# Gathering stage: splitting the second bank of weights into two rounded parts in every fourth unit

## The chip, the cores and the metric

The kernel runs on one core of a Trainium2 chip. The metric is the device time of one execution in microseconds; what is compared is the median over runs. The core has TensorE (PE, matrix products), VectorE (DVE), ScalarE (ACT), GpSimd (POOL) and SyncE (SP, which here only issues DMAs). Each engine runs its own instructions in order, and they wait for one another by semaphores. SBUF is the working memory; PSUM is the memory that TensorE writes to.

## The reference

A decoder layer for 64 sequences of 128 tokens with 128 features: self-attention, cross-attention, and a soft mixture of experts. The stage that is changed belongs to the last part:

```python
# x: 8192 tokens x 128; 64 experts (n) with 32 slots (p) each
logits = (einsum('tzd,ed->tze', x, phi_w) + phi_b).reshape(t, z, n, p)
D = softmax(logits, axis=3)                # over the slots of one expert
X_tilde = einsum('tznp,tzd->npd', D, x)    # gathers 2048 slots of 128
...
Y = einsum('tznp,npH->tzH', softmax(logits, axis=2), Y_tilde)
```

The gathering stage computes `logits`, `D` and `X_tilde`, and stores half of the logits for the last stage.

## The kernel before

Stages run one after the other: attention, cross-attention, a short preparation, **gathering** (`gather_slots`, about 603 to 1052 us of the profile), the experts, and the mixing stage.

Gathering goes over 64 tiles of 128 tokens, and over each in two **units**: unit `u` takes tile `u // 2` and half `u % 2` of the 2048 slots. So there are 128 units, and each has 1024 slots in two **banks** of 512 (16 experts each). A software pipeline with lags is written out by hand: iteration `k` works on units `k` to `k - 4`, each engine in the order of its own loop.

- TensorE: logits of unit `k` (L849, six matmuls of rounded fp32r operands: high times high, low times high, high times low, for two banks); subtraction of the maxima of unit `k - 1` in PSUM (L856, two); for unit `k - 4` the products that gather tokens into slots, summed over all tiles in four PSUM banks `slots_X`. Of these, bank 1 is one matmul in full fp32 (L863), which the trace records as two instructions. Bank 0 is three fp32r matmuls (L868 to L870), of `x2h`, `x2l` (high and low part of the tokens) and `dh`, `dl` (high and low part of the weights).
- ScalarE: copies the logits to keep, bank 1 and bank 0 (L875); the exponential `e` of unit `k - 1` (L886); for unit `k - 2` the rounded `x2h` (L895, every second unit) and `dh` (L898).
- VectorE: maxima `mx` of both banks of unit `k` (L907, L909); for unit `k - 1` sums `rsum` (L913) and reciprocals `rinv` (L917); every second unit `x2l` (L923).
- GpSimd: `dl` of unit `k - 3` (L932), then the weights `d` of unit `k - 1`, which is `e` times `rinv` (L938, both banks, 1024 columns).

`d` lies in four buffers, `dh` and `dl` in two each. In the names of the trace the stage's own tiles begin with `gather_`. In the attention stage, GpSimd's L210 adds two bands of 128x512 and its L213 adds a constant to four columns; VectorE's L359 works on 128x512 with both inputs in SBUF, and its L330 on 128x512 with one input in PSUM.

Of the kernel before, what the change touches and what calls it, by code (L numbers as in the profile page):

```python
# [18 lines left out]
ALU = mybir.AluOpType  # L19
# [3 lines left out]
F32R = mybir.dt.float32r  # L23
# [32 lines left out]
def reach(eng, sem, value):  # L56

    if not isinstance(value, int) or value > 0:
        eng.wait_ge(sem, value)  # L59
# [730 lines left out]
def gather_slots(nc, io, w, psX):  # L790
# [4 lines left out]
    TILES = TOKENS // 128  # L795
    UNITS = 2 * TILES
    KEEPS = 3
    with ExitStack() as ctx:
        st = Store(nc, ctx, "gather")
        mx = [st.sb(f"mx{i}", [128, 2, 16], F32R) for i in range(2)]  # L800
# [3 lines left out]
        dd = [st.sb(f"d{i}", [128, 2, 512]) for i in range(4)]  # L804

        x2h = [st.sb(f"x2h{i}", [128, 128], F32R) for i in range(2)]
        x2l = [st.sb(f"x2l{i}", [128, 128], F32R) for i in range(2)]
        dh = [st.sb(f"dh{i}", [128, 512], F32R) for i in range(2)]
        dl = [st.sb(f"dl{i}", [128, 512], F32R) for i in range(2)]
        keep = [st.sb(f"keep{i}", [128, SLOTS - MADE, 32]) for i in range(KEEPS)]  # L810
        psL = [st.ps(f"L{i}", [128, 2, 512]) for i in range(2)]

# [3 lines left out]
         x_made) = (  # L816
            st.sem(n) for n in ("l_made", "low_max", "mx_ready", "kept", "shifted", "e_ready", "sum_done", "rinv_ready",
                                "d_ready", "d_read", "dh_ready", "dl_ready", "x_made"))
        stored = [st.sem(f"stored{i}") for i in range(KEEPS)]
        block = ctx.enter_context(nc.Block())  # L820

        def units(k, lag):
            return [k - lag] if 0 <= k - lag < UNITS else []

        def rows(u):
            return slice(u // 2 * 128, u // 2 * 128 + 128)
# [14 lines left out]
        @block.tensor  # L841
        def _(pe):
            for k in ORDER:
                for u in units(k, 0):
                    reach(pe, e_ready, u - 1)
                    for n, (xs, ws) in enumerate(((w.xh, w.w1h), (w.xl, w.w1h), (w.xh, w.w1l))):
                        for i in range(2):
                            c = (2 * (u % 2) + i) * 512
                            ins = pe.matmul(psL[u % 2][:, i, :], xs[:, rows(u)], ws[:, c:c + 512],  # L849
                                            start=n == 0, stop=n == 2)  # L850
                    ins.then_inc(l_made, 1)
                for u in units(k, 1):
                    pe.wait_ge(mx_ready, u + 1)
                    pe.wait_ge(kept, 2 * u + 2)
                    for i in range(2):
                        ins = pe.matmul(psL[u % 2][:, i, :], w.neg_ident[:],  # L856
                                        mx[u % 2][:, i, :].unsqueeze(2).to_broadcast([128, 16, 32]), start=False,
                                        stop=True, skip_group_check=True)
                    ins.then_inc(shifted, 1)
                for u in units(k, 4):  # L860
                    t, j, first, last = u // 2, u % 2, u < 2, u >= UNITS - 2
                    pe.wait_ge(d_ready, u + 1)
                    pe.matmul(psX[:, 2 * j + 1, :], w.xres[:, rows(u)], dd[u % 4][:, 1, :], start=first, stop=last)\  # L863
                        .then_inc(d_read, 1)
                    pe.wait_ge(x2l_ready, t + 1)
                    pe.wait_ge(dl_ready, u + 1)
                    out = psX[:, 2 * j, :]
                    pe.matmul(out, x2h[t % 2][:], dh[j][:], start=first, stop=False)  # L868
                    pe.matmul(out, x2h[t % 2][:], dl[j][:], start=False, stop=False)
                    pe.matmul(out, x2l[t % 2][:], dh[j][:], start=False, stop=last).then_inc(x_made, 1)  # L870

        @block.scalar
        def _(act):
            def keep_bank(u, i):
                act.copy(keep[u % KEEPS][:, :, 16 * i:16 * i + 16],  # L875
                         psL[u % 2][:, i, :].rearrange("t (n p) -> t p n", n=16)[:, MADE:SLOTS, :]).then_inc(kept, 1)

            for k in ORDER:
                for u in units(k, 0):
                    act.wait_ge(l_made, u + 1)  # L880
                    reach(act, stored[u % KEEPS], 16 * (u // KEEPS))
                    keep_bank(u, 1)
                for u in units(k, 1):
                    act.wait_ge(shifted, u + 1)
                    reach(act, d_ready, u - 1)
                    act.activation(e[u % 2][:], psL[u % 2][:].rearrange("p i (n s) -> p i n s", n=16), ACT.Exp)\  # L886
                        .then_inc(e_ready, 1)
                for u in units(k, 0):
                    act.wait_ge(low_max, u + 1)
                    keep_bank(u, 0)  # L890
                for u in units(k, 2):
                    t, j = u // 2, u % 2
                    if j == 0:
                        reach(act, x_made, u - 2)
                        act.copy(x2h[t % 2][:], w.xres[:, rows(u)]).then_inc(x2h_ready, 1)  # L895
                    act.wait_ge(d_ready, u + 1)
                    reach(act, x_made, u - 1)
                    act.copy(dh[j][:], dd[u % 4][:, 0, :]).then_inc(dh_ready, 1)  # L898

        @block.vector  # L900
        def _(dve):
            for k in ORDER:
# [15 lines left out]
                for u in units(k, 2):  # L918
                    t = u // 2
                    if u % 2 == 0:  # L920
                        dve.wait_ge(x2h_ready, t + 1)
                        reach(dve, x_made, u - 2)
                        dve.tensor_tensor(x2l[t % 2][:], w.xres[:, rows(u)], x2h[t % 2][:], ALU.subtract)\  # L923
                            .then_inc(x2l_ready, 1)

        @block.gpsimd
        def _(pool):
            for k in ORDER:
                for u in units(k, 3):
                    pool.wait_ge(dh_ready, u + 1)  # L930
                    reach(pool, x_made, u - 1)
                    pool.tensor_tensor(dl[u % 2][:], dd[u % 4][:, 0, :], dh[u % 2][:], ALU.subtract).then_inc(dl_ready, 1)  # L932
                for u in units(k, 1):
                    pool.wait_ge(rinv_ready, u + 1)

                    reach(pool, d_read, u - 3)
                    reach(pool, dl_ready, u - 3)
                    pool.tensor_tensor(  # L938
                        dd[u % 4][:].rearrange("p i (n s) -> p i n s", n=16), e[u % 2][:],
                        rinv[u % 2][:].rearrange("p (i n) -> p i n", i=2).unsqueeze(3).to_broadcast([128, 2, 16, 32]),  # L940
                        ALU.mult).then_inc(d_ready, 1)
# [413 lines left out]
```

## Time and profile before

| | |
|---|---|
| Median of 3 runs | 1550.07 us (1549.28 to 1550.47) |
| The profiled execution | 1551.19 us, its span 1549.0 us |
| Mean granted clock of TensorE | 0.966 of 2.4 GHz |
| Busy in the span: PE, DVE, ACT, POOL | 1387.7, 1164.3, 872.3, 1151.5 us |
| Gathering: GpSimd's L938 and L932 (128 each) | 244.9 us and 165.9 us busy |
| Gathering: VectorE's L913, L907, L909, L917 (128 each) | 156.2, 88.5, 87.0, 45.2 us busy |
| Gathering: TensorE's L863 (256 records) | 130.7 us busy |

How to read the rows further down: times are microseconds from the start of the span, durations of an operation's executions are nanoseconds. PEld is TensorE's loading of weights, which runs beside its matmuls. In brackets behind a timeline row stands the engine's idle time before it and what ended that. A matmul's recorded length is longer than the distance to the next, since matmuls are pipelined; starts are what to compare. A record may start shortly before the engine's last one ends. An execution's recorded length includes time in which it was issued but held up.

### The profile page before, as it was taken

To read this page: it belongs to the slowest core of one execution; us is meant where nothing else is said; L and a number is where in the kernel's file an instruction comes from. 1 tells how busy PE (TensorE), PEld (TensorE's weight loads), DVE (VectorE), ACT (ScalarE), POOL (GpSimd) and SP (SyncE) were. 2 spreads that over 40 slices of the span, in tenths; PEclk is the share of its full clock that TensorE was granted. 3 is DMA by queue.
4 is the path that set the end of the run, shared out by engine and by line. 5 is a ranking of instruction groups with operands and counts; after the bars stand their busy time and mean duration, and the time that the engine had idled before them with its cause. 6 is when DMAs were issued, how large, how long until landed. Compare 5 with 4: busy or idle time off the path is not lost. (4 is left out here: it accounts for less than half of the span.)

```text
span 1549.0 us, 35158 instructions
## 1 busy us (share of the span) xinstructions
PE 1387.7 (90%) x12926; PEld 1114.6 (72%) x12926; DVE 1164.3 (75%) x2389; ACT 872.3 (56%) x1546; POOL 1151.5 (74%) x1028
## 2 busy tenths in 40 slices
PE   5765588888888885999999999996999999999998
PEld 4554466666666653777777777764899999999998
DVE  4997466666666665888888888885778778787885
ACT  3776244444444442676767677762566565655655
POOL 2443466666666652899999999993899999999997
PEclk9897599999999997999999999999999999999999
DMA  5110343333333314222222222221222332232231
GB/s 158 35 40 7 97 118 89 90 90 89 90 90 92 92 41 130 76 76 81 76 82 76 82 75 78 79 75 42 86 79 76 93 84 77 87 93 79 76 92 28
DMA packets 77195, 123.82 MB, mean 80 GB/s; under 512 B 8353, under 2 KB 45794, under 8 KB 77026
## 3 DMA queue, kind: packets, MB, share of 16 engines
q1 hardware_dynamic: 75426, 117.16, 24.2%
q0 software_dynamic: 1088, 4.19, 0.9%
q8 instruction: 104, 1.70, 0.5%
q14 instruction: 65, 0.53, 0.1%
q10 hardware_dynamic: 512, 0.23, 0.1%
HBM read 70.28 MB, written 51.27 MB: 78 GB/s over the span
## 5 line engine op out<-in xcount | busy, mean ns | idle before, releaser
L938 POOL TENSOR_TENSOR gather_d<-gather_e,gather_rinv 128x1024 f32<-128x1024 f32 x128 | 244.9, 1914 | 53.4 <-DVE gather_rinv L917 53.4
L1244 POOL TENSOR_TENSOR mix_c<-mix_e,mix_rinv 128x1024 f32<-128x1024 f32 x128 | 241.0, 1903 | 24.9 <-DVE mix_rinv L1211 24.9
L1171 PEld LDWEIGHTS mix_Y<-kept_phi,mix_cT 128*128 128x128 f32 x2048 | 248.1, 192 | 9.0
L1171 PE MATMUL mix_Y<-kept_phi,mix_cT 128*128 128x128 f32 x2048 | 249.0, 275 | 0.0
L1187 ACT COPY mix_cT<-mix_T 128x1024 f32<-128x1024 f32 x128 | 128.6, 1005 | 170.1 <-PE mix_T L1178 170.1
L1208 DVE TENSOR_REDUCE mix_sums<-mix_e 128x16 f32<-128x1024 f32 x128 | 152.6, 1193 | 85.3 <-ACT mix_e L1191 83.0
L717 POOL TENSOR_TENSOR cross_kd<-cross_pack,kept_consts 128x624 fp32r<-128x624 f32 x128 | 155.3, 1233 | 42.1 <-DMA cross_pack<-cross_halves 40.9
L913 DVE TENSOR_REDUCE gather_rsum<-gather_e 128x32 f32<-128x1024 f32 x128 | 156.2, 1220 | 26.7 <-ACT gather_e L886 26.7
L932 POOL TENSOR_TENSOR gather_dl<-gather_d,gather_dh 128x512 fp32r<-128x512 f32 x128 | 165.9, 1296 | 0.0
L875 ACT COPY gather_keep<-gather_L 128x256 f32<-128x256 f32 x256 | 94.7, 370 | 105.5 <-PE gather_L L849 98.7
L595 ACT ACTIVATE cross_pT<-cross_P 77x1024 f32<-77x1024 f32 x128 | 123.5, 1015 | 49.0 <-PE cross_P L536 49.0
L1178 PE MATMUL mix_T<-kept_consts,mix_c 128*128 128x128 f32 x1024 | 134.6, 275 | 5.1 <-POOL mix_c L1244 5.0
L1255 POOL TENSOR_TENSOR mix_less<-mix_read,mix_high 128x1024 f32<-128x1024 f32 x64 | 122.4, 1913 | 19.3 <-DVE mix_high L1224 19.1
L886 ACT ACTIVATE gather_e<-gather_L 128x1024 f32<-128x1024 f32 x128 | 131.2, 1025 | 8.3 <-PE gather_L L856 0.9
L645 DVE TENSOR_REDUCE cross_mx<-cross_S 128x8 fp32r<-128x624 f32 x128 | 102.9, 804 | 39.5 <-PE cross_S L518 39.5
L863 PE MATMUL slots_X<-gather_d,kept_xres 128*128 128x512 f32 x256 | 130.7, 592 | 0.0
L1178 PEld LDWEIGHTS mix_T<-kept_consts,mix_c 128*128 128x128 f32 x1024 | 117.6, 143 | 6.4 <-POOL mix_c L1244 6.4
L907 DVE TENSOR_REDUCE gather_mx<-gather_L 128x16 fp32r<-128x512 f32 x128 | 88.5, 691 | 32.7 <-PE gather_L L849 23.7
L868 PE MATMUL slots_X<-gather_dh,gather_x2h 128*128 128x512 f32 x128 | 101.3, 792 | 2.9 <-DVE gather_x2l L923 1.5
L723 POOL TENSOR_TENSOR cross_veps<-cross_mv,kept_eps 128x1 f32<-128x1 f32 x64 | 12.1, 189 | 120.8 <-DVE cross_mv L659 120.8
L898 ACT CAST gather_dh<-gather_d 128x512 fp32r<-128x512 f32 x128 | 79.8, 623 | 32.1 <-PE slots_X L870 20.0
L849 PE MATMUL gather_L<-second_w1h,kept_xh 128*128 128x512 f32 x256 | 82.0, 401 | 12.8 <-ACT gather_e L886 9.0
(188 smaller groups left out, 3171.5 us busy)
## 6 DMA issues: line engine op xcount, KB each, us to landing
kept_logits<-gather_keep SPq DMA_DIRECT2D x128, 256.0 KB, 2.0
mix_read<-kept_logits SPq DMA_DIRECT2D x64, 512.0 KB, 3.7
cross_halves<-cross_qk SPq DMA_DIRECT2D x32, 412.0 KB, 2.9
cross_pack<-cross_halves SPq DMA_DIRECT2D x64, 128.0 KB
cross_pack<-cross_halves SPq DMA_DIRECT2D x32, 206.0 KB
cross_pack<-cross_halves SPq DMA_DIRECT2D x64, 78.0 KB
attn_xTg<-in_xT SPq DMA_DIRECT2D x16, 256.0 KB, 2.8
kept_xres<-in_x POOLq DMA_DIRECT2D x4, 1024.0 KB, 12.3
```

Of the source, the lines that this page charges most:

```text
L595: ins = act.activation(pT[n % 2][0:J, hs, :, :], psP[:, hs, :, :], ACT.Exp)
L717: pool.tensor_tensor(kd[n % 2][:, q], keys[:, q].to_broadcast([128, 2, 4, JP]), w.own.unsqueeze(1).unsqueeze(3).to_broadcast([128, 2, 4, J ...
L863: pe.matmul(psX[:, 2 * j + 1, :], w.xres[:, rows(u)], dd[u % 4][:, 1, :], start=first, stop=last)\
L886: act.activation(e[u % 2][:], psL[u % 2][:].rearrange("p i (n s) -> p i n s", n=16), ACT.Exp)\
L913: dve.tensor_reduce(rsum[u % 2][:].rearrange("p (i n) -> p i n", i=2), e[u % 2][:], X, ALU.add)\
L932: pool.tensor_tensor(dl[u % 2][:], dd[u % 4][:, 0, :], dh[u % 2][:], ALU.subtract).then_inc(dl_ready, 1)
L938: pool.tensor_tensor(dd[u % 4][:].rearrange("p i (n s) -> p i n s", n=16), e[u % 2][:], rinv[u % 2][:].rearrange("p (i n) -> p i n", i=2). ...
L1171: ins = pe.matmul(psY[t % 2][:, 0:128], cT[u % 2][:, c, :], w.yk[:, 8 * (u % 2) + c, :], start=(u % 2 == 0 and c == 0), stop=(u % 2 == 1 a ...
L1178: ins = pe.transpose(psT[:, c, :], cc[u % 2][:, 2 * c:2 * c + 2, :], w.ident)
L1187: act.copy(cT[u % 2][:], psT[:]).then_inc(cT_ready, 1)
L1208: dve.tensor_reduce(sums[u % 2][:], e[u % 2][:], X, ALU.add).then_inc(sum_done, 1)
L1244: pool.tensor_tensor(cc[u % 2][:], e[u % 2][:], rinv[u % 2][:].unsqueeze(2).to_broadcast([128, 16, EXPERTS]), ALU.mult)\
```

## The change

In every fourth unit (u = 3, 7, ... 127, all in the second half of their tile) bank 1 is gathered as bank 0 is: ScalarE makes a rounded high part `eh` of the bank's weights, VectorE subtracts it from them and gets the low part `el`, and TensorE does three fp32r matmuls in place of the one in fp32. `eh` and `el` have one buffer each; three semaphores are new. The three matmuls come after those of bank 0.

```diff
@@ gather_slots @@
+    SPLIT = 4
...
+        def split(u):
+
+            return u % SPLIT == SPLIT - 1
...
@@ block.tensor, unit k - 4 @@
                     pe.wait_ge(d_ready, u + 1)
-                    pe.matmul(psX[:, 2 * j + 1, :], w.xres[:, rows(u)], dd[u % 4][:, 1, :], start=first, stop=last)\
-                        .then_inc(d_read, 1)
+                    out = psX[:, 2 * j + 1, :]
+                    if not split(u):
+                        pe.matmul(out, w.xres[:, rows(u)], dd[u % 4][:, 1, :], start=first, stop=last)\
+                            .then_inc(d_read, 1)
...
                     pe.matmul(out, x2l[t % 2][:], dh[j][:], start=False, stop=last).then_inc(x_made, 1)
+                    if split(u):
+                        out = psX[:, 2 * j + 1, :]
+                        pe.wait_ge(el_ready, u // SPLIT + 1)
+                        pe.matmul(out, x2h[t % 2][:], eh[:], start=first, stop=False)
+                        pe.matmul(out, x2h[t % 2][:], el[:], start=False, stop=False)
+                        pe.matmul(out, x2l[t % 2][:], eh[:], start=False, stop=last).then_inc(split_read, 1)
...
@@ block.scalar, after dh of unit k - 2 @@
+                for u in units(k, 3):
+                    if split(u):
+                        reach(act, split_read, u // SPLIT)
+                        act.copy(eh[:], dd[u % 4][:, 1, :]).then_inc(eh_ready, 1)
...
@@ block.vector, after x2l of unit k - 2 @@
+                for u in units(k, 3):
+                    if split(u):
+                        dve.wait_ge(eh_ready, u // SPLIT + 1)
+                        reach(dve, split_read, u // SPLIT)
+                        dve.tensor_tensor(el[:], dd[u % 4][:, 1, :], eh[:], ALU.subtract).then_inc(el_ready, 1)
...
@@ block.gpsimd, before d of unit k - 1 @@
-                    reach(pool, d_read, u - 3)
+                    reach(pool, d_read, straight(u - 3))
+                    reach(pool, el_ready, max(u - 3, 0) // SPLIT)
```

`straight(n)` counts the units among the first `n` that are not split. ScalarE (before `x2h`) and VectorE (before `x2l`) wait for `split_read` too, before they overwrite the tokens' parts.

VectorE's instructions around the end of iteration 6, before. `mx` are the maxima, `rsum` and `rinv` the sums and reciprocals of the softmax:

```order
L913 TENSOR_REDUCE gather_rsum<-gather_e 128x32 [waits gather_rinv_ready,gather_e_ready]
L917 RECIPROCAL gather_rinv<-gather_rsum 128x32 [waits gather_d_ready,gather_sum_done]
L923 TENSOR_TENSOR gather_x2l<-kept_xres,gather_x2h 128x128 [waits gather_x_made,gather_x2h_ready]
L907 TENSOR_REDUCE gather_mx<-gather_L 128x16 [waits gather_shifted,gather_l_made]
L909 TENSOR_REDUCE gather_mx<-gather_L 128x16 [waits gather_kept]
L913 TENSOR_REDUCE gather_rsum<-gather_e 128x32 [waits gather_rinv_ready,gather_e_ready]
```

And VectorE at the same place now:

```order
L934 TENSOR_REDUCE gather_rsum<-gather_e 128x32 [waits gather_rinv_ready,gather_e_ready]
L938 RECIPROCAL gather_rinv<-gather_rsum 128x32 [waits gather_d_ready,gather_sum_done]
L945 TENSOR_TENSOR gather_x2l<-kept_xres,gather_x2h 128x128 [waits gather_x_made,gather_x2h_ready]
L951 TENSOR_TENSOR gather_el<-gather_d,gather_eh 128x512 [waits gather_eh_ready]
L928 TENSOR_REDUCE gather_mx<-gather_L 128x16 [waits gather_shifted,gather_l_made]
L930 TENSOR_REDUCE gather_mx<-gather_L 128x16 [waits gather_kept]
L934 TENSOR_REDUCE gather_rsum<-gather_e 128x32 [waits gather_rinv_ready,gather_e_ready]
```

`el` stands between `x2l` and the maxima of the next unit. All 32 do, since `el` is in iteration u + 3, which is even, as those with `x2l` are.

ScalarE in the same iteration, before:

```order
L875 COPY gather_keep<-gather_L 128x16x16 [waits gather_low_max]
L895 CAST gather_x2h<-kept_xres 128x128 [waits gather_x_made]
L898 CAST gather_dh<-gather_d 128x512 [waits gather_x_made,gather_d_ready]
L875 COPY gather_keep<-gather_L 128x16x16 [waits gather_stored1,gather_l_made]
L886 ACTIVATE gather_e<-gather_L 128x1024 [waits gather_d_ready,gather_shifted]
```

And ScalarE at the same place now:

```order
L891 COPY gather_keep<-gather_L 128x16x16 [waits gather_low_max]
L912 CAST gather_x2h<-kept_xres 128x128 [waits gather_x_made]
L915 CAST gather_dh<-gather_d 128x512 [waits gather_x_made,gather_d_ready]
L919 CAST gather_eh<-gather_d 128x512
L891 COPY gather_keep<-gather_L 128x16x16 [waits gather_stored1,gather_l_made]
L902 ACTIVATE gather_e<-gather_L 128x1024 [waits gather_d_ready,gather_shifted]
```

`eh` stands behind `dh`, in front of the copy of the next unit's logits.

TensorE around unit 3, the first that is split (iteration 7), where `slots_X` is the gathered sum; before:

```order
L856 MATMUL gather_L<-gather_mx,kept_neg_ident 128x512 x2
L863 MATMUL slots_X<-gather_d,kept_xres 128x512
L868 MATMUL slots_X<-gather_dh,gather_x2h 128x512
L869 MATMUL slots_X<-gather_dl,gather_x2h 128x512
L870 MATMUL slots_X<-gather_dh,gather_x2l 128x512
L849 MATMUL gather_L<-second_w1h,kept_xh 128x512 x2
```

And TensorE at the same place now:

```order
L864 MATMUL gather_L<-gather_mx,kept_neg_ident 128x512 x2
L878 MATMUL slots_X<-gather_dh,gather_x2h 128x512
L879 MATMUL slots_X<-gather_dl,gather_x2h 128x512
L880 MATMUL slots_X<-gather_dh,gather_x2l 128x512
L884 MATMUL slots_X<-gather_eh,gather_x2h 128x512
L885 MATMUL slots_X<-gather_el,gather_x2h 128x512
L886 MATMUL slots_X<-gather_eh,gather_x2l 128x512
L857 MATMUL gather_L<-second_w1h,kept_xh 128x512 x2
```

L863 (now L873) is gone from this iteration, and L884 to L886 stand behind the three matmuls of bank 0. GpSimd's order is the same as before.

## Rows read from the trace of the kernel before

**Rows 1.** Busy time by stretches (stretch, length, PE, PEld, DVE, ACT, POOL, clock, DMA).

```profile
740.00:840.00 100.00, 100.00 (x386) 72.34 (x385) 86.63 (x134) 69.89 (x134) 93.47 (x61) 1.00 0.21 80
```

**Rows 2.** Waits, 640 to 1040 us (engine, line, releaser: total, times, longest).

```profile
POOL gather_d L938 <- DVE gather_rinv L917: 25.9, 119, 0.2
```

**Rows 3.** Timeline, one iteration (start us, length us, engine, line, operation, tiles).

```profile
801.01 1.30 POOL L932 TENSOR_TENSOR gather_dl<-gather_d,gather_dh 128x512 fp32r<-128x512 f32 x1
...
801.14 0.63 PE L849 MATMUL gather_L<-second_w1h,kept_xh 128*128 128x512 f32 x2
...
801.40 0.62 ACT L898 CAST gather_dh<-gather_d 128x512 fp32r<-128x512 f32 x1
...
802.09 0.35 DVE L917 RECIPROCAL gather_rinv<-gather_rsum 128x32 f32<-128x32 f32 x1
...
802.36 0.23 DVE L923 TENSOR_TENSOR gather_x2l<-kept_xres,gather_x2h 128x128 fp32r<-128x128 f32 x1
802.52 1.91 POOL L938 TENSOR_TENSOR gather_d<-gather_e,gather_rinv 128x1024 f32<-128x1024 f32 x1 [0.21 <-DVE gather_rinv L917]
802.54 0.59 PE L856 MATMUL gather_L<-gather_mx,kept_neg_ident 128*128 128x512 f32 x2
...
802.74 0.69 DVE L907 TENSOR_REDUCE gather_mx<-gather_L 128x16 fp32r<-128x512 f32 x1
...
802.97 1.02 PE L863 MATMUL slots_X<-gather_d,kept_xres 128*128 128x512 f32 x2
803.17 1.02 ACT L886 ACTIVATE gather_e<-gather_L 128x1024 f32<-128x1024 f32 x1
803.35 0.68 DVE L909 TENSOR_REDUCE gather_mx<-gather_L 128x16 fp32r<-128x512 f32 x1
...
804.23 1.22 DVE L913 TENSOR_REDUCE gather_rsum<-gather_e 128x32 f32<-128x1024 f32 x1 [0.20 <-ACT gather_e L886]
804.30 0.39 PE L870 MATMUL slots_X<-gather_dh,gather_x2l 128*128 128x512 f32 x1
...
804.53 0.62 PE L849 MATMUL gather_L<-second_w1h,kept_xh 128*128 128x512 f32 x2
...
805.48 0.35 DVE L917 RECIPROCAL gather_rinv<-gather_rsum 128x32 f32<-128x32 f32 x1
...
805.91 1.91 POOL L938 TENSOR_TENSOR gather_d<-gather_e,gather_rinv 128x1024 f32<-128x1024 f32 x1 [0.23 <-DVE gather_rinv L917]
```

**Rows 4.** Executions of L932 (count, shortest/median/longest ns, first and last).

```profile
L932 POOL TENSOR_TENSOR gather_dl<-gather_d,gather_dh x128: 1258/1298/1307, 614.5 to 1049.2; 128x512 fp32r<-128x512 f32 x128
```

**Rows 5.** Executions of L923, and the timeline at the stage's end.

```profile
L923 DVE TENSOR_TENSOR gather_x2l<-kept_xres,gather_x2h x64: 227/229/1306, 612.5 to 1045.0; 128x128 fp32r<-128x128 f32 x64
...
1044.86 1.26 POOL L932 TENSOR_TENSOR gather_dl<-gather_d,gather_dh 128x512 fp32r<-128x512 f32 x1
1044.96 1.31 DVE L923 TENSOR_TENSOR gather_x2l<-kept_xres,gather_x2h 128x128 fp32r<-128x128 f32 x1
1046.08 1.96 POOL L938 TENSOR_TENSOR gather_d<-gather_e,gather_rinv 128x1024 f32<-128x1024 f32 x1
```

**Rows 6.** Executions of L359, and the timeline near its longest.

```profile
L359 DVE SCALAR_TENSOR_TENSOR attn_band<-attn_a,attn_band x16: 656/658/1259, 22.0 to 137.1; 128x512 f32<-128x512 f32 x16
...
21.43 0.68 DVE L330 TENSOR_TENSOR attn_vp<-attn_V,first_b 128x512 f32<-128x512 f32 x1
21.46 1.27 POOL L210 TENSOR_TENSOR attn_band<-attn_band 128x512 f32<-128x512 f32 x1 [5.45 <-DVE attn_band L323]
22.02 1.26 DVE L359 SCALAR_TENSOR_TENSOR attn_band<-attn_a,attn_band 128x512 f32<-128x512 f32 x1
```

**Rows 7.** Executions of L213, and the timeline around one of them.

```profile
L213 POOL TENSOR_TENSOR attn_veps<-attn_mv,kept_eps x16: 198/556/557, 39.6 to 148.5; 128x4 f32<-128x4 f32 x16
...
100.21 0.66 DVE L359 SCALAR_TENSOR_TENSOR attn_band<-attn_a,attn_band 128x512 f32<-128x512 f32 x1
100.37 0.56 POOL L213 TENSOR_TENSOR attn_veps<-attn_mv,kept_eps 128x4 f32<-128x4 f32 x1 [2.09 <-DVE attn_mv L355]
```

More of the change, by code:

```diff
@@ L809, in gather_slots @@
         dl = [st.sb(f"dl{i}", [128, 512], F32R) for i in range(2)]
+        eh = st.sb("eh", [128, 512], F32R)
+        el = st.sb("el", [128, 512], F32R)
         keep = [st.sb(f"keep{i}", [128, SLOTS - MADE, 32]) for i in range(KEEPS)]
@@ L818, in gather_slots @@
                                 "d_ready", "d_read", "dh_ready", "dl_ready", "x_made"))
+        eh_ready, el_ready, split_read = (st.sem(n) for n in ("eh_ready", "el_ready", "split_read"))
         stored = [st.sem(f"stored{i}") for i in range(KEEPS)]
@@ L894, in _ @@
                         reach(act, x_made, u - 2)
+                        reach(act, split_read, max(u - 2, 0) // SPLIT)
                         act.copy(x2h[t % 2][:], w.xres[:, rows(u)]).then_inc(x2h_ready, 1)
@@ L922, in _, with straight @@
                         reach(dve, x_made, u - 2)
+                        reach(dve, split_read, max(u - 2, 0) // SPLIT)
                         dve.tensor_tensor(x2l[t % 2][:], w.xres[:, rows(u)], x2h[t % 2][:], ALU.subtract)\
                             .then_inc(x2l_ready, 1)
+                for u in units(k, 3):
[3 more added lines that the diff above has]
+                        dve.tensor_tensor(el[:], dd[u % 4][:, 1, :], eh[:], ALU.subtract).then_inc(el_ready, 1)
         @block.gpsimd
         def _(pool):
+            def straight(n):
+                return n - n // SPLIT if n > 0 else 0
             for k in ORDER:
```

## The prediction

> **What bounds the kernel now.** I read the view of busy time by stretch first, to see which engines the gathering stage leaves idle. In 100 us of its steady part TensorE is busy throughout at a granted clock of 1.00 (the 2.4 GHz level), GpSimd for 93.5 us, VectorE for 86.6, ScalarE for 69.9 [rows 1]. A busy TensorE need not be its limit, so I read the timeline of one iteration for gaps in its matmuls [rows 3]. One iteration goes from the first L849 at 801.14 to the next at 804.53, 3.39 us; `d` has the same distance (802.52 to 805.91). Six L849 fill 801.14 to 802.54 (1.40, so 0.233 each), two L856 0.43, then L863, L868 and L869 take 802.97 to 804.30. L870 to L849 is 0.23 again. At 0.233 for each fp32r matmul of 128x512, L863 has 1.33 - 0.47 = 0.86 to itself, and no pause is left. The one other thing L849 could wait for, ScalarE's exponential, ends at 803.17 + 1.02 = 804.19, 0.34 early.
>
> GpSimd stands right behind. Per unit it does one `d` (L938, 1.91) [rows 3] and one `dl` (L932, 1.26 at the least, recorded as 1.30 where it follows `d` directly and its start lies 0.04 before the end of `d`) [rows 3, 4], 3.17 of 3.39. The remaining 0.2 is the wait for VectorE's `rinv`: 25.9 us in 119 waits [rows 2]. So TensorE sets the pace, and a loss of GpSimd of more than 0.2 per unit is not absorbed.
>
> The gap matters for a second reason. VectorE's `x2l` (L923) runs at 802.36 to 802.59, just where GpSimd has finished `dl` (802.31) and just before it starts `d` (802.52) [rows 3]. Of its 64 executions most take 0.229, but the longest 1.306 [rows 5]. That one was issued at 1044.96, 0.10 after GpSimd had begun a `dl`, and it ended at 1046.27, 0.15 after that `dl` (1046.12) [rows 5]. The attention stage shows the same with the width that the change adds: L359, 128x512 with both inputs in SBUF, takes 0.658, but 1.259 when issued at 22.02 inside GpSimd's L210 (21.46 to 22.73); it ended at 23.28, 0.55 after GpSimd. L330, of which one input is in PSUM, ran at 21.43 beside the same L210 in its 0.68 [rows 6]. The other way round, GpSimd's L213 (four elements a row, minimum 0.198) takes 0.56 when it is issued at 100.37 behind VectorE's L359 (100.21) [rows 7]. So a VectorE instruction with two SBUF inputs and a GpSimd instruction exclude one another for their whole length, and the first keeps the other out.
>
> The Trainium skill (SBUF — State Buffer, section "Who interferes with whom") states that as a rule: a VectorE instruction with two SBUF inputs contends with a GpSimd instruction that reads SBUF, and issue order decides who blocks. By that rule, the rows above agree. It speaks against this change, whose new VectorE instruction is of that kind.
>
> **The change, part by part.** In 32 of 128 units:
>
> *TensorE* loses L863 (0.86) and gets three fp32r matmuls (3 x 0.233 = 0.70): -0.16 a time, -5.1 us in all, if TensorE stays the bound [rows 3]. The Trainium skill (TensorE: Matmul & The Clock Gate, section "Back-to-back issue gap") gives about 216 ns for 512 columns; by that figure the estimate would be -0.21 a time and -6.8. The rows' 0.233 is what this stage shows.
>
> *ScalarE* gets one more cast of 128x512 (`eh`), 0.62 like L898. It has 30 us in 100 free. In the iteration shown it would follow L898 (801.40) at about 801.92, ScalarE's next starting some 0.10 before the last ends (L898 recorded to 802.02), and end at 802.54; the next copy is due at about 802.74. Cost nothing by itself, but it fixes when `el` can start: 802.54 and a hand-off of 0.04 (e ends 804.19, VectorE's L913 starts 804.23) make 802.58 [rows 3].
>
> *GpSimd* gets only one more wait, for an `el` of two iterations ago: nothing. PE's new wait is costed below. No DMA is moved.
>
> *VectorE* gets `el`, 128x512, both inputs in SBUF. Queued behind it are the two maxima of the next unit (L907, L909), then the sum and the reciprocal, for which GpSimd's next `d` waits. It is issued at 802.58 at the earliest; GpSimd's `d` started at 802.52. So by these rows `el` comes 0.06 late, is shut out until `d` ends at 804.43, and then gets in between `d` and `dl`, as `x2l` did between two GpSimd instructions in [rows 5]. I take the price as follows, from the end of that `d`: `el` ends 0.55 later (as L359 did), and L907 may start 0.08 before that: 0.47. L907 to L909 0.61 (802.74 to 803.35). L909 to L913 0.60 (0.68 less the same 0.08). L913 to L917 1.25 (804.23 to 805.48). L917 0.35, and 0.08 to the start of `d` (805.83 to 805.91). Sum 3.36 [rows 3, 6]. In that time GpSimd has had one `dl` and stood idle otherwise, where it now waits 0.2. From there it works without a pause until the next `el`: four `d` (7.64) and three `dl` (3.78), 11.42, and 0.02 for two `x2l` that slip in between (in [rows 5] the `d` behind one ended at 1048.04, 1.92 after the `dl`). Together 14.80 us for four units, instead of 4 x 3.39 = 13.56: **+1.24 per group of four.**
>
> Can the others follow? VectorE's reciprocals for the next three units come every 2.73 plus what `x2l` has to wait for `dl` (about 0.5 once on the way), GpSimd takes 3.17 a unit, so yes, with some 0.1 to 0.2 to spare. TensorE now stops for `el` in front of its last three matmuls. From there: 0.04, 0.70, two whole iterations 6.78, six L849 1.40, L856 to the exponential 0.63, that 1.02, 0.04, L913 to L917 1.25, 0.35, 0.08, the next `d` 1.91, `el` 0.55: 14.75. That ring is as long as GpSimd's, so neither hides the other's gain: TensorE's -0.16 is lost in its own stop of about 1.4 us.
>
> Between 32 `el` lie 31 such groups: 31 x 1.24 = +38.4. At the stage's end the last unit's three matmuls (0.70) come after `dl`, which itself is some 0.5 late, less a part of L863: +1. Sum **+39.4**. The profiled execution took 1551.2 (span 1549.0), which gives 1590.6; the median of the runs is 1.1 lower, 1550.1, which gives 1589.5: **1590**. The bounds of that case: `el` as quick as `x2l` behind its release (0.15, less 0.4 a group) gives 1578; 0.1 lost at two hand-overs of the port in each group gives 1596, and `rinv` late by 0.3 once a group 1599.
>
> **The rivals.**
>
> *VectorE comes first, faster than before.* The 0.06 between 802.58 and 802.52 is all that decides who holds the port. If ScalarE is a little earlier, or a GpSimd start as recorded is not yet its claim to the port, `el` runs at 802.52 to 803.15, `d` is 0.48 late, and GpSimd's 0.2 a unit makes that up before the next `el`. L907 starts 0.4 late, but L909, which ended at 804.03, is wanted by the L856 at 804.53 + 1.40 = 805.93 only, 1.9 later. Then TensorE stays the bound: -5.1 + 1 = -4, 1546. For it: how close the race is. Against it: once GpSimd has won one race, `x2l` waits for `dl` too, and `el` behind it comes some 0.1 later against `d`, so one loss keeps the slow order, while a win must be repeated 32 times. It decides from 0.06 us on. 18%.
>
> *Some races each way*: 1555 to 1580. 8%.
>
> *GpSimd keeps the port over `dl` too*, since `dl` is ready when `d` ends. In [rows 5] the next `d` had been ready as well (it started without a pause, at 1046.08), and `x2l` got in; that speaks against. It would add another 1.26 a group: 31 x 2.50 + 1 = +79, 1629. 6%.
>
> **How the numbers follow.** Main case 68%, its own range 1578 to 1600. The fast case's 18% can't be left out together with the 6%, so the range goes from 1545 to 1600, and leaves out the 6% and a little more. A measurement of this kernel tells about 0.2% (3.1 us) from no change. The fast case lies at -0.25%, so I give two thirds of it to faster: faster 0.13, same 0.06, slower 0.81.
>
> **What would show it.** Right: `el` recorded at about 2.4 to 2.5 us instead of 0.7, ending 0.55 after a `d`; L907 behind it some 2 us late; iterations of TensorE 3.39, 3.39, 3.39 and about 4.6; TensorE's wait named after `el` (32 times, some 1.4); `x2l` with a median well over 0.229 in half of its cases; GpSimd busy the same in sum. Wrong: `el` at 0.6 to 0.7 in all 32, and `d` starting behind it, which is the fast rival; `el` ending behind a `dl`, which is the slow one. If `el` overlapped `d` undelayed, the whole reading of the port would fall, and the time would be 1546 for another reason.

## The result, and the profile after

| | before | changed |
|---|---|---|
| Median, same chip | 1549.97 us (1549.28 to 1554.57, 6 runs) | 1593.85 us (1593.15 to 1599.35, 6 runs) |
| Profiled execution, its span | 1551.19, 1549.0 us | 1599.35, 1597.2 us |
| Busy in the span: PE, DVE, ACT, POOL | 1387.7, 1164.3, 872.3, 1151.5 us | 1393.7, 1239.6, 889.6, 1164.0 us |

The changed kernel takes 1.0287 times as long (95% interval 1.0272 to 1.0302), 43.9 us more. The two profiled executions differ by 48.2. Where these lie can be read from starts. Gathering begins at 600.5 before and at 604.1 after, so 3.7 us arose ahead of any changed line and say nothing on the change. From there to the first instruction of the experts (1052.2, now 1100.1) it is 451.8 before and 496.0 after: 44.2 more. The rest of the kernel adds 0.3.

Busy time of the same stretch as in [rows 1] (stretch, length, PE, PEld, DVE, ACT, POOL, clock, DMA), after:

```profile
740.00:840.00 100.00, 90.21 (x353) 65.48 (x352) 95.21 (x126) 66.68 (x127) 85.87 (x54) 1.00 0.19 70
```

TensorE is no longer busy throughout; VectorE's share has risen from 86.6 to 95.2, but that "busy" holds time in which an instruction was issued and held up. The granted clock is 1.00 in both, the 2.4 GHz level, so it has no part in this. GpSimd's share falls because fewer units go through in 100 us.

Executions of `el` (L951), `x2l` (L945) and `eh` (L919), after (count, shortest/median/longest ns), and TensorE's and GpSimd's waits from 640 to 1040 us:

```profile
L951 DVE TENSOR_TENSOR gather_el<-gather_d,gather_eh x32: 1746/2419/2422, 637.7 to 1096.4; 128x512 fp32r<-128x512 f32 x32
L945 DVE TENSOR_TENSOR gather_x2l<-kept_xres,gather_x2h x64: 226/256/2032, 615.4 to 1091.9; 128x128 fp32r<-128x128 f32 x64
L919 ACT CAST gather_eh<-gather_d x32: 611/612/615, 637.1 to 1095.8; 128x512 fp32r<-128x512 f32 x32
...
POOL gather_d L970 <- DVE gather_rinv L938: 46.5, 30, 3.3
...
PE slots_X L884 <- DVE gather_el L951: 34.1, 27, 2.5
```

Where GpSimd waited 25.9 us for `rinv` in 119 short waits [rows 2], it now waits 46.5 in 30 long ones. One group of four units, after, in the rows that answer to [rows 3]:

```profile
801.04 0.63 PE L857 MATMUL gather_L<-second_w1h,kept_xh 128*128 128x512 f32 x2
...
801.82 0.61 ACT L919 CAST gather_eh<-gather_d 128x512 fp32r<-128x512 f32 x1
...
802.26 0.23 DVE L945 TENSOR_TENSOR gather_x2l<-kept_xres,gather_x2h 128x128 fp32r<-128x128 f32 x1
802.43 1.91 POOL L970 TENSOR_TENSOR gather_d<-gather_e,gather_rinv 128x1024 f32<-128x1024 f32 x1
...
802.47 2.42 DVE L951 TENSOR_TENSOR gather_el<-gather_d,gather_eh 128x512 fp32r<-128x512 f32 x1
...
804.30 1.74 POOL L963 TENSOR_TENSOR gather_dl<-gather_d,gather_dh 128x512 fp32r<-128x512 f32 x1
804.81 0.68 DVE L928 TENSOR_REDUCE gather_mx<-gather_L 128x16 fp32r<-128x512 f32 x1
804.94 0.50 PE L884 MATMUL slots_X<-gather_eh,gather_x2h 128*128 128x512 f32 x1 [1.22 <-DVE gather_el L951]
...
805.75 0.62 PE L857 MATMUL gather_L<-second_w1h,kept_xh 128*128 128x512 f32 x2
...
807.25 0.35 DVE L938 RECIPROCAL gather_rinv<-gather_rsum 128x32 f32<-128x32 f32 x1
...
807.68 1.92 POOL L970 TENSOR_TENSOR gather_d<-gather_e,gather_rinv 128x1024 f32<-128x1024 f32 x1 [1.64 <-DVE gather_rinv L938]
...
817.13 0.23 DVE L945 TENSOR_TENSOR gather_x2l<-kept_xres,gather_x2h 128x128 fp32r<-128x128 f32 x1
817.29 1.91 POOL L970 TENSOR_TENSOR gather_d<-gather_e,gather_rinv 128x1024 f32<-128x1024 f32 x1
817.34 2.42 DVE L951 TENSOR_TENSOR gather_el<-gather_d,gather_eh 128x512 fp32r<-128x512 f32 x1
```

`el` is issued at 802.47, 0.04 behind `d`. It is held until `d` ends at 804.34, and ends at 804.89, 0.55 later. `dl`, issued at 804.30, is held by it in turn (1.74 instead of 1.30). The maxima stand behind `el`, TensorE stands for it 1.22 us, and GpSimd is idle for 1.64 before its next `d`. The next `el` is at 817.34: 14.87 us for four units, where four took 13.55.

### The profile page after: what moved, and what is told of

Read it like the earlier page. It is cut to its first block and busy times, and to the rows that moved or that the text cites. A ratio compares the mean times of both kernels' runs of the same rounds, so it can differ in the third digit from the quotient of the medians.

```text
span 1597.2 us, 35499 instructions
## 1 busy us (share of the span) xinstructions
PE 1393.7 (87%) x12958; PEld 1118.8 (70%) x12958; DVE 1239.6 (78%) x2421; ACT 889.6 (56%) x1578; POOL 1164.0 (73%) x1028
## 5 line engine op out<-in xcount | busy, mean ns | idle before, releaser
L963 POOL TENSOR_TENSOR gather_dl<-gather_d,gather_dh 128x512 fp32r<-128x512 f32 x128 | 178.7, 1397 | 0.0
L873 PE MATMUL slots_X<-gather_d,kept_xres 128*128 128x512 f32 x192 | 98.9, 597 | 0.0
L928 DVE TENSOR_REDUCE gather_mx<-gather_L 128x16 fp32r<-128x512 f32 x128 | 85.7, 669 | 15.6 <-PE gather_L L857 15.4
L857 PE MATMUL gather_L<-second_w1h,kept_xh 128*128 128x512 f32 x256 | 82.1, 402 | 13.1 <-ACT gather_e L902 9.6
L878 PE MATMUL slots_X<-gather_dh,gather_x2h 128*128 128x512 f32 x128 | 89.2, 697 | 3.4 <-POOL gather_dl L963 3.4
```

## The experiments

Theory: `el` is shut out by a `d` that GpSimd issues just before it, since both need the same way to SBUF (called the port here); all else follows from that. Which of the two is issued first is called their race. Rivals: the changed kernel is slower because `el`, `eh` and their waits make the orders of VectorE and ScalarE longer, whoever has the port; or because TensorE stops for `el`. Runs of one group share a chip and the runs of the kernel before. The edits are against the changed kernel. Costs are against the kernel before on the same chip; the changed kernel's is 43.9 us.

**One SBUF input (`e1_one_input`).** A reduction over one element takes the subtraction's place at the same 128x512, with the same waits. `eh` is not subtracted; that is left out of the computation.

```diff
-   dve.tensor_tensor(el[:], dd[u % 4][:, 1, :], eh[:], ALU.subtract).then_inc(el_ready, 1)
+   dve.tensor_reduce(el[:], dd[u % 4][:, 1, :].unsqueeze(2), X, ALU.max).then_inc(el_ready, 1)
```

> The changed kernel, but el is made by a VectorE instruction of the same size with one SBUF input (a tensor_reduce over an axis of length 1 of the same weights), so the subtraction of eh is left out and bank 1 of the split units gets wrong low parts; all waits, the cast and the matmuls stay. Theory (el is shut out by GpSimd's d because it has two SBUF inputs): el takes about 0.7 us instead of 2.42, the group of four falls from 14.87 to 13.40 us, the time to about 1546. Rival (VectorE's extra 0.7 us of work and the place in its queue are what costs): the time stays within 5 us of 1594, whatever the recorded length of el.

Measured: 1546.28 us (1545.73 to 1547.64), ratio to before 0.9958 (0.9943 to 0.9973). Its timeline, beside `d`:

```profile
807.94 1.92 POOL L970 TENSOR_TENSOR gather_d<-gather_e,gather_rinv 128x1024 f32<-128x1024 f32 x1 [0.21 <-DVE gather_rinv L938]
807.99 0.69 DVE L951 TENSOR_REDUCE gather_el<-gather_d 128x512 fp32r<-128x512 f32 x1
```

The same place, 0.05 behind `d` (0.04 and 0.05 in the rows above), the same width, and neither is held. An instruction more on VectorE and on ScalarE costs nothing here; what costs came with the subtraction and its second SBUF input. The operation is another one too, so the next run keeps it and changes only who is first. The rest shows what TensorE's saving is worth when nothing takes it: groups of 13.35 instead of 13.55. One race was still lost here, by the small `x2l`, which kept its two SBUF inputs:

```profile
739.50 2.03 DVE L945 TENSOR_TENSOR gather_x2l<-kept_xres,gather_x2h 128x128 fp32r<-128x128 f32 x1
```

It made two groups of 15.30 and 13.13, 1.7 us over.

**GpSimd waits for `el` (`e14_gpsimd_waits`).** One wait is moved from two iterations later to the same one, so that `el` always has the port first.

```diff
-   reach(pool, el_ready, max(u - 3, 0) // SPLIT)
+   for v in units(k, 3):
+       if split(v):
+           pool.wait_ge(el_ready, v // SPLIT + 1)
```

> The changed kernel with one wait moved and nothing else: GpSimd's d of unit k - 1 waits for the el of the same iteration (32 times), where it waited for that of two iterations before. So el always has the port first. Port theory: el 0.63 to 0.69 us instead of 2.42; the d behind it starts at about 803.2 instead of 802.4 on the old grid, 0.7 late, and GpSimd's work for a group of four is 4 x 1.91 + 4 x 1.26 + 0.7 for el + 0.1 for the hand-overs = 13.5, against TensorE's 13.4: group 13.4 to 13.6 instead of 14.87, time 1547 to 1555, about as the kernel before and 40 below the changed one, although a wait is added. Rival (the cost lies in VectorE's and ScalarE's longer order and not in who has the port): el stays over 1.3 us or the added wait costs its own length, 31 x 0.7 = 22 on top, so 1594 to 1615.

Measured: 1552.51 (1551.32 to 1557.72), ratio 1.0009 (0.9998 to 1.0019). `el`, and one group of it:

```profile
L951 DVE TENSOR_TENSOR gather_el<-gather_d,gather_eh x32: 676/678/1810, 632.8 to 1049.3; 128x512 fp32r<-128x512 f32 x32
...
794.70 0.65 DVE L945 TENSOR_TENSOR gather_x2l<-kept_xres,gather_x2h 128x128 fp32r<-128x128 f32 x1
795.27 0.68 DVE L951 TENSOR_TENSOR gather_el<-gather_d,gather_eh 128x512 fp32r<-128x512 f32 x1
...
796.18 1.92 POOL L972 TENSOR_TENSOR gather_d<-gather_e,gather_rinv 128x1024 f32<-128x1024 f32 x1 [0.98 <-DVE gather_el L951]
```

An added wait of 0.98 us takes 42.5 us off the cost, from 43.9 to 1.4. The instructions of all engines and their orders are as in it; only who comes first has changed. This is the clearest of the runs: the cost was neither the work nor the fact that TensorE needs `el`. Groups are 13.54, and now GpSimd sets them: its distance from `d` to `d` is 3.11 without a pause, four of them 12.44, and 1.04 and 0.06 for the two places where it stands back.

**The products one iteration later (`e6_products_later`), and `el` made but not used (`e10_el_unused`).** The first moves the block of TensorE's three matmuls (and the wait for `el`) from `units(k, 4)` to `units(k, 5)`; the second drops it and leaves TensorE as before, so that `eh` and `el` are mere extra work. Without TensorE's matmuls nothing counts `split_read`: the waits for it go, ScalarE waits for the last `el` before it overwrites `eh`, and GpSimd counts L873 in every unit again. Of the second, in part:

```diff
-                    if not split(u):
+                    if True:
                         pe.matmul(out, w.xres[:, rows(u)], dd[u % 4][:, 1, :], start=first, stop=last)\
...
-                    if split(u):
-                        out = psX[:, 2 * j + 1, :]
-                        pe.wait_ge(el_ready, u // SPLIT + 1)
...
```

> Only TensorE's order is changed: the three matmuls of a split unit stand one iteration later, behind the six of the next unit's logits, so el is there 1.4 us before they need it. Theory (two rings of nearly the same length, TensorE's of 14.75 and GpSimd's of 14.80 by the sum, 14.87 measured): the wait of TensorE for el disappears, but the maxima that stand behind el on VectorE hold L864 and GpSimd's reciprocal as before; the group stays at 14.7 to 14.9, the time at 1588 to 1594. Rival (TensorE's stop of 1.2 us in front of these matmuls is the cost): the time falls to 1550 or below.

> eh and el are made where the changed kernel makes them, but TensorE works as in the kernel before (one fp32 matmul for bank 1 in every unit) and reads neither. Theory: VectorE's hold-up alone reaches GpSimd by the late reciprocal; without any wait of TensorE for el the group of four is GpSimd's ring, 14.74 to 14.80, so about +37 to +39 us against the kernel before, 1587 to 1589. Rival (the cost comes through TensorE's wait for el): about 1550.

Measured: 1589.19 (1587.73 to 1591.11), 1.0236 (1.0216 to 1.0255), and 1588.35 (1585.62 to 1590.54), 1.0228 (1.0207 to 1.025). VectorE in the second, over 100 us, and its `el`:

```profile
740.00:840.00 100.00, 95.39 (x357) 65.82 (x356) 98.99 (x131) 66.82 (x131) 89.02 (x55) 1.00 0.20 74
...
L944 DVE TENSOR_TENSOR gather_el<-gather_d,gather_eh x32: 1816/2401/2416, 632.9 to 1085.4; 128x512 fp32r<-128x512 f32 x32
```

No product uses this `el`, and the kernel is still 36 us slower than before. So TensorE's stop is not the cause. By a ring I mean the chain of instructions from one `el` to the next in which each waits for the one before. Both runs give the ring of VectorE and GpSimd alone: 14.70 a group. The 14.87 of the changed kernel is TensorE's own ring, 0.17 longer.

**The high part earlier (`e5_high_part_earlier`).** ScalarE makes `eh` one iteration earlier, right behind `dh` of the same unit, so that it is long done when VectorE comes to `el`.

```diff
                     act.copy(dh[j][:], dd[u % 4][:, 0, :]).then_inc(dh_ready, 1)
-                for u in units(k, 3):
                     if split(u):
                         reach(act, split_read, u // SPLIT)
```

> One edit to the changed kernel: ScalarE makes eh one iteration earlier (right behind dh of the same unit), so el no longer waits for it and can start as soon as x2l lets it, up to 0.06 us earlier than the 0.04 by which it now comes behind GpSimd's d. Theory (issue order decides who holds the port): if el's record starts before that of d, it takes 0.7, d is recorded 0.4 to 0.5 longer, and the time falls to about 1546; if it still starts behind, it takes 2.4 and the time stays at 1594. Rival (GpSimd has precedence whenever it is near, or VectorE's load is the cost): 1594 in either case.

Measured: 1551.86 (1550.24 to 1557.17), ratio 1.0000 (0.9986 to 1.0015). A race that is won, and one that is lost:

```profile
810.63 0.23 DVE L944 TENSOR_TENSOR gather_x2l<-kept_xres,gather_x2h 128x128 fp32r<-128x128 f32 x1
810.77 0.68 DVE L950 TENSOR_TENSOR gather_el<-gather_d,gather_eh 128x512 fp32r<-128x512 f32 x1
810.79 2.44 POOL L969 TENSOR_TENSOR gather_d<-gather_e,gather_rinv 128x1024 f32<-128x1024 f32 x1 [0.21 <-DVE gather_rinv L937]
...
739.72 1.91 POOL L969 TENSOR_TENSOR gather_d<-gather_e,gather_rinv 128x1024 f32<-128x1024 f32 x1 [0.21 <-DVE gather_rinv L937]
739.75 2.03 DVE L944 TENSOR_TENSOR gather_x2l<-kept_xres,gather_x2h 128x128 fp32r<-128x128 f32 x1
741.59 1.31 POOL L962 TENSOR_TENSOR gather_dl<-gather_d,gather_dh 128x512 fp32r<-128x512 f32 x1
741.71 1.75 DVE L950 TENSOR_TENSOR gather_el<-gather_d,gather_eh 128x512 fp32r<-128x512 f32 x1
```

`el` is now recorded 0.02 ahead of `d`, runs in 0.68, and `d` is held for 0.53. Issued 0.02 ahead or 0.04 behind: that is the difference of about 43 us between two kernels that do the same work. The time fell between the two that were expected, since most races were won and not all. Groups are 13.35, as with one input. The gain over the kernel before is eaten by what follows two lost races: `x2l` at 739.75 came 0.03 behind `d`, and the two groups there took 15.35 and 15.68 (4.3 us together over 13.35); another loss at 944.39 cost 1.5.

Not all of the 4.3 is the race. TensorE stood for `el` for 2.48 us, and then ran at a lower granted clock (stretch, length, PE, PEld, DVE, ACT, POOL, clock, DMA):

```profile
744.00:748.00 4.00, 4.00 (x12) 3.06 (x11) 2.67 (x5) 1.37 (x4) 1.76 (x1) 0.59 0.18 66
```

That is the 1.2 GHz level for most of the stretch. The six L857 took 2.56 us (744.66 to 747.22) instead of 1.40, and the two matmuls before them 0.81 instead of 0.47: about 1.5 us. The changed kernel had the same stop of 2.48 us at 760.34 and its clock stayed at 1.00; why, these runs don't show.

Why `x2l` started 0.2 us later than usual at 739.75 stays open, but it isn't chance. From there to the next late one (844.10), and from that to the late `el` at 944.39, VectorE has 143 recorded instructions each time. The same `x2l`, the 19th, is as late in the changed kernel (756.59) and in `e1_one_input` (739.50), with the same 143 to the next late one. Whether the lateness costs anything depends on what GpSimd is doing at that moment.

**Both waits (`e13_both_waits`).** `e5_high_part_earlier`, with GpSimd's `d` waiting for the `x2l` and the `el` of its own iteration.

```diff
-   reach(pool, el_ready, max(u - 3, 0) // SPLIT)
+   for v in units(k, 2):
+       if v % 2 == 0:
+           pool.wait_ge(x2l_ready, v // 2 + 1)
+   for v in units(k, 3):
+       if split(v):
+           pool.wait_ge(el_ready, v // SPLIT + 1)
```

> e5_high_part_earlier with two waits more: GpSimd's d of unit k - 1 waits in every second iteration for that iteration's x2l, and in every fourth for its el, so that neither race can be lost. Port theory: el 0.63 to 0.69 in all 32, x2l 0.23 in all 64, all groups 13.35 to 13.45, none of 14 to 16 as e5_high_part_earlier had at 726 to 755 and at 944 to 970. That saves 31 x 0.16 to 0.21 = 5 to 6.5 less 1 at the end against the kernel before: 1545 to 1548, ratio 0.997 to 0.999. Rival (e5_high_part_earlier's long groups come from something else than the lost port, or the added waits cost GpSimd 0.1 a time): groups of 13.5 to 13.6 and a time of 1550 to 1556.

Measured: 1564.0 (1562.45 to 1565.37), ratio 1.0074 (1.0061 to 1.0087). A miss: 1545 to 1548 was expected, and it is above the rival's range too. GpSimd and `x2l` in one group:

```profile
790.75 1.28 POOL L962 TENSOR_TENSOR gather_dl<-gather_d,gather_dh 128x512 fp32r<-128x512 f32 x1
...
791.09 1.08 DVE L944 TENSOR_TENSOR gather_x2l<-kept_xres,gather_x2h 128x128 fp32r<-128x128 f32 x1
...
792.40 1.92 POOL L974 TENSOR_TENSOR gather_d<-gather_e,gather_rinv 128x1024 f32<-128x1024 f32 x1 [0.38 <-DVE gather_x2l L944]
...
799.68 1.92 POOL L974 TENSOR_TENSOR gather_d<-gather_e,gather_rinv 128x1024 f32<-128x1024 f32 x1 [1.01 <-DVE gather_el L950]
```

I had priced a wait as the port's hold (0.53). It costs 1.06: GpSimd is idle for `el`'s whole length and for the semaphore's way. With 0.42 for the wait for `x2l`, the group is 12.44 + 1.06 + 0.42 = 13.92, as measured. GpSimd is the bound then, works behind schedule, so `x2l` (issued 791.09) falls inside `dl`, waits for its end (1.08 instead of 0.23), and `d` waits for `x2l`: the added wait makes the lateness that it then pays for. No version that I ran beats the kernel before and computes the same.

**`el` in other places.** `e4_el_before_x2l` puts the blocks of `eh` and `el` ahead of those of `x2h`/`dh` and `x2l`. `e7_el_after_maxima` has `eh` early as in `e5_high_part_earlier` and moves the block of `el` to between the maxima and the sum.

```diff
@@ e7, block.vector @@
+                for u in units(k, 3):
+                    if split(u):
+                        dve.wait_ge(eh_ready, u // SPLIT + 1)
+                        reach(dve, split_read, u // SPLIT)
+                        dve.tensor_tensor(el[:], dd[u % 4][:, 1, :], eh[:], ALU.subtract).then_inc(el_ready, 1)
                 for u in units(k, 1):
                     dve.wait_ge(e_ready, u + 1)
```

> The same operations as in the changed kernel, in another order: ScalarE makes eh before x2h and dh, and VectorE makes el before x2l, right behind the reciprocal. Theory of the port: el is issued about 0.15 us before GpSimd's d instead of 0.04 behind it, takes 0.7, d starts 0.5 late and GpSimd's slack of 0.2 a unit takes that up; x2l has to follow and may be shut out by d in its turn for 1.9 us (128x128, both inputs in SBUF), which would cost about as much as now. So 1546 if x2l follows el directly, 1590 if d gets in between. Rival (VectorE's load): 1590 in both cases with el at 0.7.

> eh one iteration earlier as in the run beside it, and el moved in VectorE's queue from behind x2l to between the two maxima and the sum. There GpSimd is already 1.6 us into d's 1.91. Theory of the port: el is shut out for the rest of d only, so it is recorded with about 0.9 to 1.0 instead of 2.42, the reciprocal is some 0.7 late instead of 2.0, and GpSimd's slack of 0.2 a unit takes that up within the four units: group 13.4 to 13.6, time 1546 to 1553. Rival (what costs is VectorE's extra work and any wait of it, wherever it stands): above 1580.

Measured: 1588.5 (1586.53 to 1589.04), 1.0228 (1.0207 to 1.0249), and 1551.94 (1550.22 to 1556.23), 0.9999 (0.9988 to 1.0011). The first, then the second:

```profile
852.48 1.28 POOL L963 TENSOR_TENSOR gather_dl<-gather_d,gather_dh 128x512 fp32r<-128x512 f32 x1
...
853.00 1.30 DVE L943 TENSOR_TENSOR gather_el<-gather_d,gather_eh 128x512 fp32r<-128x512 f32 x1
853.72 2.37 POOL L970 TENSOR_TENSOR gather_d<-gather_e,gather_rinv 128x1024 f32<-128x1024 f32 x1
854.23 2.00 DVE L950 TENSOR_TENSOR gather_x2l<-kept_xres,gather_x2h 128x128 fp32r<-128x128 f32 x1
```

```profile
805.26 1.91 POOL L969 TENSOR_TENSOR gather_d<-gather_e,gather_rinv 128x1024 f32<-128x1024 f32 x1
...
806.57 1.15 DVE L934 TENSOR_TENSOR gather_el<-gather_d,gather_eh 128x512 fp32r<-128x512 f32 x1
807.14 1.74 POOL L962 TENSOR_TENSOR gather_dl<-gather_d,gather_dh 128x512 fp32r<-128x512 f32 x1
```

In the first, `el` gets the port behind `dl`, and the small `x2l` is then shut out by the whole `d`: a quarter of the work, the same price, 14.70 a group. In the second `el` is issued late in a `d`, waits 0.60, ends 0.55 after it, and holds `dl`. It loses its race every time, but for little: 13.50 a group, one unlucky pair at 941 to 970 of 14.77 and 13.89. A lost race costs what is left of the other engine's instruction, and what waits behind it: here the maxima stood behind `el` no more, and the run doesn't tell the two apart.

**Every eighth unit (`e12_every_eighth`), and `el` by GpSimd (`e2_low_part_by_gpsimd`).**

```diff
-    SPLIT = 4
+    SPLIT = 8
```

```diff
@@ e2, block.gpsimd, behind dl; block of el gone from block.vector, reach(pool, el_ready, ...) gone, eh early as in e5 @@
+                    if split(u):
+                        pool.wait_ge(eh_ready, u // SPLIT + 1)
+                        reach(pool, split_read, u // SPLIT)
+                        pool.tensor_tensor(el[:], dd[u % 4][:, 1, :], eh[:], ALU.subtract).then_inc(el_ready, 1)
```

> The changed kernel with every eighth unit split instead of every fourth: 16 el. Theory (each el costs its own stop, since TensorE's ring is set anew by each): half the cost, 16 x 1.3 = +21 us, 1571. Rival (the cost per el depends on whether GpSimd has caught up with its lag before the next, which with four units it just does not): with eight units it catches up, and each el costs less than 0.8: below 1563.

> el is made by GpSimd, behind dl, instead of VectorE (eh one iteration earlier, so that it doesn't wait). VectorE does nothing new and no exclusion is left between the two but for x2l. Theory: the group is GpSimd's own work, 4 x 3.17 + 1.26 = 13.94 and 0.02 for x2l, against TensorE's 13.40: 32 x 0.4 = +12 us against the kernel before, 1562. Rival (VectorE makes el better, since GpSimd is the fuller engine): above 1594.

Measured: 1571.8 (1570.88 to 1575.16), 1.0125 (1.0103 to 1.0148), and 1560.19 (1559.93 to 1561.53), 1.0048 (1.003 to 1.0067).

```profile
L951 DVE TENSOR_TENSOR gather_el<-gather_d,gather_eh x16: 1806/2416/2419, 646.5 to 1069.5; 128x512 fp32r<-128x512 f32 x16
```

```profile
740.00:840.00 100.00, 98.75 (x385) 71.42 (x384) 89.36 (x131) 71.86 (x139) 100.00 (x66) 1.00 0.20 76
...
L961 POOL TENSOR_TENSOR gather_el<-gather_d,gather_eh x32: 1276/1334/1348, 632.8 to 1059.8; 128x512 fp32r<-128x512 f32 x32
```

Half as many `el` cost half as much (20.4 against 43.9 us): each loses its race, and each delay is paid in full. Done by GpSimd, the low part takes 1.33 us, twice as long as an unhindered one on VectorE (0.68), and GpSimd is busy 100 us in 100. It still costs only 8.8 us, some 35 less than the changed kernel: a longer instruction that isn't held is cheaper than a short one that is shut out.

## Why the prediction was right

**The time.** 1590 was forecast, 1593.85 measured, inside the range and inside the main case's own 1578 to 1600. Slower was given 0.81.

**What bounds.** Right: of the 0.2 us that GpSimd had to spare per unit 0.13 is left once in a group (817.16 to 817.29), and TensorE stands for `el`.

**The race.** Right, and as close as it looked. The sum had `el` at 0.06 behind `d`; it was 0.04. That it fell on this side was partly luck: the sum can't be trusted to some hundredths, and `el` 0.06 earlier wins (`e5_high_part_earlier`). The 18% for the other side had said so. `eh` starts 0.53 after `dh` (801.29 to 801.82); [rows 3] had given 0.52. `el` ended 0.55 after `d`, exactly as L359 behind L210 in [rows 6]. That `el` and `d` shut one another out, and that who is first decides, the trace of before could only suggest; `e1_one_input` and `e14_gpsimd_waits` show it. The Trainium skill (SBUF — State Buffer, section "Who interferes with whom") has the rule; its condition of two SBUF inputs is what `e1_one_input` took away (0.69 us beside a running `d`), and its "Issue order, not op shape, decides who blocks" is what `e5_high_part_earlier` and `e14_gpsimd_waits` turned round.

**The group.** 1.24 over before was forecast, 1.31 measured (14.87). From the end of `d` to the next `d` the sum had 3.36; it is 3.34 (804.34 to 807.68). The two rings came out in the other order. GpSimd's, forecast 14.80, is 14.70 by `e6_products_later` and `e10_el_unused`. The term that was too large is the 3.17 for a `d` and a `dl`: they follow each other at 3.11 (3.18 where an `x2l` slips in), since each starts some 0.04 before the last one's recorded end, which I had taken off `dl` only. TensorE's, forecast 14.75, is 14.87. There the term is the three matmuls at 0.70: from the end of `el` (804.89) to L857 (805.75) are 0.86, where I had 0.04 + 0.70. The first matmul behind the stop takes until 805.28, 0.34 from its start and not 0.233. So the ring that I had called equal is the one that binds, by 0.17. The two mistakes have opposite signs, and the longer ring came out within 0.07 of the sum: that it is so near is partly luck. TensorE's own saving was a little more than forecast, 0.20 a group in `e1_one_input` (13.55 to 13.35) against 0.16; in the changed kernel it is lost either way.

**The rest of the 44.** From the `x2l` beside the first `el` (633.03 before, 637.50 after) to that beside the 31st (1039.43, 1084.74) the profiled executions take 406.41 and 447.24: 30 groups, 40.8 more, where the sum gives 37.2. Of the 3.6, 30 x 0.08 = 2.4 are the term above (14.87 against the 14.80 that the sum used, and 13.55 against 13.56 before), and 1.2 the group of 16.78 with the short one of 14.20 behind it; another uneven pair (14.96, 14.77) adds nothing. In the group of 16.78 `x2l` too lost its race:

```profile
756.56 1.91 POOL L970 TENSOR_TENSOR gather_d<-gather_e,gather_rinv 128x1024 f32<-128x1024 f32 x1
756.59 2.03 DVE L945 TENSOR_TENSOR gather_x2l<-kept_xres,gather_x2h 128x128 fp32r<-128x128 f32 x1
758.43 1.31 POOL L963 TENSOR_TENSOR gather_dl<-gather_d,gather_dh 128x512 fp32r<-128x512 f32 x1
758.54 1.75 DVE L951 TENSOR_TENSOR gather_el<-gather_d,gather_eh 128x512 fp32r<-128x512 f32 x1
```

The last group and the end give 2.6 (forecast 1.24 + 1), and the first iterations 0.8, for which the sum had no term.

**The traces it named.** `el` 2.42 (forecast 2.4 to 2.5); L928 behind it 3.77 after the iteration's first L857 instead of 1.60 in [rows 3], so 2.17 late (forecast 2); TensorE's iterations 4.71, 3.39, 3.38, 3.39 (forecast 4.6 and three of 3.39); its wait for `el` 1.26 on average (34.1 in 27; forecast 1.4); `x2l` at 0.23 in the iterations with an `el` and at about 0.64 in the others, which makes its median 0.256. One was wrong: GpSimd's busy time isn't the same in sum but 12.5 us more. The `dl` behind each `el` is held and recorded 0.44 longer (1.74 against 1.30), 14 us in 32; records that overlap at more places than before take a little off.

**The rivals.** "VectorE comes first" is what `e5_high_part_earlier` makes true by moving one cast. Its price of 1546 was met where `el` can't lose (`e1_one_input`, 1546.28, in which one `x2l` did), but the kernel that does the whole computation loses two races in the steady part and lands at 1551.86. My remark that a win must be repeated 32 times while one loss keeps the slow order was half right: each win has to be made anew, but after a loss the trace of that kernel found back to 13.35 within two groups. "GpSimd keeps the port over `dl` too" never showed: each held VectorE instruction got in at the next boundary between two of GpSimd's. The doubt that a GpSimd start as recorded may not yet be its claim was justified, though not for `d`. Near the end of `e12_every_eighth` a `dl` is recorded right behind a `d`, and `x2l` 0.11 behind that `dl`:

```profile
1064.94 1.45 POOL L963 TENSOR_TENSOR gather_dl<-gather_d,gather_dh 128x512 fp32r<-128x512 f32 x1
...
1065.05 0.23 DVE L945 TENSOR_TENSOR gather_x2l<-kept_xres,gather_x2h 128x128 fp32r<-128x128 f32 x1
```

`x2l` isn't held, and `dl` is (1.45 instead of 1.30). Five more runs have this at the same place, with 0.06 to 0.08; in the kernel before `x2l` lost there at 0.10 [rows 5]. So next to a `dl` that follows a `d` without a pause, recorded starts within 0.1 us don't tell who has the port.

## What to carry to other kernels

Before a VectorE instruction with two SBUF inputs is added beside a busy GpSimd, read from the timeline which of the two is issued first and by how much; if GpSimd is, charge what is left of its instruction and everything that is queued behind VectorE's, not the instruction's own length. A margin of some hundredths of a microsecond is no margin: a stray delay of 0.2 us turned races round in several of these runs. An instruction with one SBUF input, an earlier operand, or a wait that lets the short one go first took nearly the whole loss away here, but each wait costs the engine about twice what a mere hold does, and it must not stand in a ring that is already late.

## What the runs showed of the hardware

- Beside a `d` that had waited for `rinv`, a recorded start 0.01 or 0.02 us ahead of GpSimd's won the port, one 0.03 or more behind lost it. Beside a `dl` recorded right behind a `d`, starts 0.06 to 0.11 behind it still won in six runs, and one 0.10 behind lost.
- A held VectorE instruction ends a fixed time after GpSimd's: 0.55 for 128x512, about 0.15 for 128x128 (756.59 + 2.03 against 756.56 + 1.91). GpSimd's `d` that is held by an `el` issued 0.02 before it takes 2.44 instead of 1.91, 0.53 more for an instruction of 0.68.
- Letting GpSimd wait by a semaphore for the same `el` cost it 1.04 to 1.06.
- The first matmul of 128x512 behind a stop of TensorE took 0.34 to the next one's start, at a granted clock of 1.00, where those in a row take 0.233.
- After a stop of TensorE of 2.48 us the granted clock fell to 0.59 over 4 us in one run and stayed at 1.00 in another.
- Where no wait hid it, a VectorE instruction started 0.1 to 0.2 us late after every 143 recorded ones, at the same instructions in several kernels. What causes it isn't known.
